# First attention: value products in groups of four, one block later, and ten probability tiles instead of six

## What is computed

```
s1 = einsum('bhtd,bhsd->bhts', q1, k1) * scale + mask     # causal mask
s2 = einsum('bhtd,bhsd->bhts', q2, k2) * scale + mask
diff = softmax(s1) - lam * softmax(s2)
out  = einsum('bhts,bhsd->bhtd', diff, v)                 # 16 heads, v of 32 columns
```

## Time and profile before

| | |
|---|---|
| median of three runs | 972.34 us |
| the profiled execution, its own time | 969.42 us |
| its span | 967.4 us |
| first value product of the first attention, last one | 89.8 us, 415.2 us |
| PE busy | 858.3 us, 89% |
| DVE, ACT, POOL busy | 534.6, 457.4, 450.4 us |

### The profile page before, as it was taken

One profiled execution on the slowest core, in us unless ns is written; L12 is line 12 of the kernel. 1 busy time (PEld: TensorE's weight loads), 2 busy tenths in 40 slices (PEclk: granted clock), 3 DMA queues, 4 the chain that ended last, 5 costly groups with the idle time before them and its releaser, 6 DMA issues. The chain is left out here.

```text
span 967.4 us, 13868 instructions
## 1 busy us (share of the span) xinstructions
PE 858.3 (89%) x4106; PEld 427.3 (44%) x4106; DVE 534.6 (55%) x1498; ACT 457.4 (47%) x981; POOL 450.4 (47%) x893
## 2 busy tenths in 40 slices
PE   3838999999999999979955989898879999999994
PEld 2322433334333333336721233332257777777773
DVE  3738676776766766146366666664024444444445
ACT  1512555555655565722230465665524444444442
POOL 1831646646463443442130233333228677777774
PEclk9966999999999999968885799999779999999998
DMA  5484320000000000010075541112000000000001
GB/s 188 149 259 103 79 67 2 2 2 2 2 2 2 2 2 2 1 38 1 1 218 174 145 138 52 52 51 84 22 30 1 0 0 0 1 0 0 0 1 43
DMA packets 39137, 46.29 MB, mean 48 GB/s; under 512 B 5386, under 2 KB 31339, under 8 KB 39070
## 3 DMA queue, kind: packets, MB, share of 16 engines
q1 hardware_dynamic: 39076, 45.56, 16.3%
HBM read 30.05 MB, written 15.20 MB: 47 GB/s over the span
## 5 line engine op out<-in xcount | busy, mean ns | idle before, releaser
L619 DVE CUSTOM_DVE_ANT_0 ps<-ps,keep 128x512 f32<-128x512 f32 (+3 forms) x384 | 188.7, 500 | 117.7 <-PE ps L487 114.8
L575 ACT ACTIVATE top<-ps 128x512 f32<-128x512 f32 (+3 forms) x384 | 174.7, 491 | 140.7 <-PE ps L498 139.0
L487 PE MATMUL ps<-mid 96*128 96x512 bf16 (+3 forms) x576 | 191.2, 353 | 35.3 <-PEq L898 15.3
L498 PE MATMUL ps<-mid 99*128 99x512 bf16 (+3 forms) x576 | 187.9, 339 | 17.4 <-ACT mid L575 14.3
L518 PE MATMUL ps<-top,mid 128*64 128x512 f32 (+3 forms) x768 | 170.2, 513 | 0.7
L498 PEld LDWEIGHTS ps<-mid 99*128 99x128 bf16 x576 | 56.5, 101 | 212.6 <-ACT top L575 114.8
L1301 PE MATMUL ps<-xp,wp 128*128 128x512 f32 (+1 forms) x600 | 144.7, 390 | 0.0
L575 ACT ACTIVATE mid<-ps 128x512 f32<-128x512 f32 (+1 forms) x192 | 87.3, 490 | 91.4 <-PE ps L518 50.7
L1301 PEld LDWEIGHTS ps<-xp,wp 128*128 128x128 f32 (+1 forms) x600 | 111.9, 187 | 24.9 <-issue 0.5
L735 POOL TENSOR_SCALAR_AFFINE_SELECT top<-top 128x128 f32<-128x128 f32 x256 | 73.1, 298 | 103.5 <-ACT top L575 101.6
L1438 DVE SCALAR_TENSOR_TENSOR a<-th,ps 128x512 f32<-128x512 f32 (+1 forms) x50 | 34.4, 688 | 115.4 <-ACT th L1367 115.4
(11 more groups left out here) (204 smaller groups left out, 1003.5 us busy)
## 6 DMA issues: line engine op xcount, KB each, us to landing
mid<-part_scratch SPq DMA_DIRECT2D x9, 1152.0 KB, 8.5
part_scratch<-top SPq DMA_DIRECT2D x18, 384.0 KB, 3.4
top<-in_w SPq DMA_DIRECT2D x16, 396.0 KB, 3.9
part_scratch<-top SPq DMA_DIRECT2D x18, 256.0 KB, 3.4
mid<-part_scratch SPq DMA_DIRECT2D x9, 384.0 KB, 4.1
top<-in_w SPq DMA_DIRECT2D x8, 384.0 KB, 4.7
part_scratch<-top SPq DMA_DIRECT2D x18, 128.0 KB, 3.3
keep<-in_x SPq DMA_DIRECT2D x1, 1024.0 KB, 5.5
```

Source lines behind the costliest of these rows:

```text
L487: ins = nc.tensor.matmul(bank[:, 0:w], queries(pair, m)[0:PARTS, i * P:(i + 1) * P], keys(pair, m)[0:PARTS, c * 512:c * 512 + w], start=Tr ...
L498: nc.tensor.matmul(ps[:, ST_BANK + n % AHEAD, 0:w], keys(pair, m)[0:STACK, j * P:(j + 1) * P], queries(pair, m)[0:STACK, q0:q0 + w], start ...
L575: nc.scalar.activation(pr[:, n % RING, 0:w], ps[:, ST_BANK + n % AHEAD, 0:w], ACT.Exp, scale=0.25).then_inc(p_ready, 1)
L619: ins = nc.vector.tensor_tensor_reduce(bank, bank, msk[:, 512 - w:512], -1.0 if low else 1.0, 3e38 if low else -3e38, ALU.add, ALU.min if ...
```

## The change

The first attention gets ten tiles of `pr` instead of six and groups of four value products instead of two. A group is issued at the steps n = 5, 9, 13, ... and holds the blocks n - 5 to n - 2; before, it was issued at n = 2, 4, 6, ... and held n - 2 and n - 1. The four products left at the end are issued behind the loop. The second attention keeps its numbers (`RING` 6, `VGROUP` 4, `LAG` 0). Nothing changes on the other engines.

```diff
-                RING = 6
-                VGROUP = 2 if first else 4
+                RING = 10 if first else 6
+                VGROUP = 4
+                LAG = 1 if first else 0
...
-                            if n > 0 and n % VGROUP == 0:
-                                for done in range(n - VGROUP, n):
+                            if n > LAG and n % VGROUP == LAG:
+                                for done in range(n - LAG - VGROUP, n - LAG):
                                     value_step(done)
```

## The result

The changed kernel takes 994.67 us (median of 4 runs, 992.92 to 998.55); the kernel before 970.48 us, the median of its three earlier runs and one more of 966.97. The ratio of the mean times is 1.026 with a 95% interval of 1.021 to 1.031: slower by 24 us. The forecast was 996, from 984 to 1006. The profiled execution took 998.55 us with a span of 996.5, so it is 29.1 us longer than the one of before.

What follows compares the result with a forecast made beforehand. PE alone bounds the first attention. Per pair -1.5 + 2.05 + 1.17 + 0.15 = +1.87 us, +29.9 over 16 pairs; less 0.8 and 4.4, +24.7 on 969.42 gives 994.1; with 2.9 for the median, forecast 996, range 984 to 1006.

Steps and rivals of the forecast that it cites:

- The switch: First attention, PE between bf16 and value products: 0.25 us per group, paid once per four; 1.5 us per pair saved.
- The copies: First attention, ACT's copies at steps 9 and 1 delay exponentials PE needs: 1.0, 0.84 and 0.2, together 2.05 us per pair.
- The gaps: First attention, bf16 steps behind groups of four: PE waits for ACT, two score blocks ahead at most; 1.17 us per pair.
- DVE's bank at step 21: First attention, step 21: the maximum product waits for the bank of the one three before; 0.15 us per pair.
- PE's busy share near 85%: Expected sign in the profile after: PE's busy share in the first attention's windows, with the clock at 1.00.
- The masks: First attention, pairs with quantisation: later issue gives POOL's masks more time; 0.87 us for each of five, 4.4 us saved.
- POOL would no longer release L518: Expected sign in the profile after: POOL no longer a releaser of L518, the value products, in the first attention.
- The ends: First attention's first pair and loop end: no late half to copy, -0.8 us; four products left, 0.6 us, within rounding.
- Rival 4: First attention: PE's clock falls as PE idles 3.4 of 22.4 us per pair; 27 us on top, 1023; chance 0.04.
- Rival 1: First attention: nothing takes the place of what is removed, ACT and DVE have room; 944 us; chance 0.03.
- Rival 2: First attention: the copies' wait is hidden and only the gaps between groups stay; 963 us; chance 0.03.
- Rival 3: First attention: only the copies cost, the gaps are filled; 975 us, or 972 if the first copy is cheap; chance 0.05.

Runs made afterwards that it cites:

- the first experiment: Against the changed kernel, each copy L584 of the first attention stands one exponential later in ACT's order; 974.07 us, ratio 1.007 to the kernel before.

## Why the prediction was right, point by point

**The switch.** Right: 0.09 us ahead of a group and 0.16 behind, once per four products. Six groups fewer save 1.5 us per pair.

**The copies.** Right. At step 11 the prediction had 1.0 us, the trace 0.99; at step 3 it had 0.84, the trace 0.83 (312.76 to 313.59); at step 5 0.2 against 0.20. That it is the copy's place and not the group's length is shown by two kernels that differ in that alone, once with groups of four (22.31 to 20.99 us per pair) and once with groups of two (22.48 to 20.64).

**The gaps.** Right. The trace has 0.31 and 0.09 behind step 13, 0.24 and 0.04 behind step 17, 0.31 and 0.10 behind step 21, and 0.14 us for DVE's bank at step 21: 1.23 us against 1.32. (For that bank I had written 0.15, though the two times beside it, 1.2 and 1.16, differ by 0.04 only: the size was right, its working was not complete.) All waits of a pair sum to 3.25 us, and 20.50 - 1.5 + 3.25 = 22.25 stands against the 22.31 measured.

One sign did not come: PE's busy share near 85%. The window shows 92%, 44.09 of 48 us. PE idles 3.25 of 22.31 us from start to start, 15%, but a matmul's modelled end lies past the point where the next one could start (0.39 us long at 512 columns, where the next starts after 0.23), so a part of each wait counts as busy.

**The masks.** Right in effect: all pairs have one length. Wrong in what would show it. I wrote that POOL would no longer release L518; the waits still list it, and not less than before. From 120 to 425 us:
```profile
PEld ps L519 <- POOL top L736: 11.7, 45, 0.3
```
In the window of the earlier trace rows, 120 to 400 us, it is 10.7 us and 41 times against 10.5 and 29. The weight load is free well before the group is due, and what the profile names is the last event before it. From the end of the bf16 product's columns to the group are 0.09 to 0.11 us in all six groups of the pair above. The line tells of PEld's idle time, not of PE's. Before, the 0.87 us lay at the groups of steps 22, 0 and 2 (233.56, 235.16 and 236.67 us), whose masks stood behind POOL's steps L752 and L755 of 1.26 and 1.04 us. The relief needs no lag: without it, too, all pairs have one length, 21.30 us.

**The ends.** Mis-sized. I gave the last pairs the same cost as all others, 1.87 us each. Over the 14 pairs up to step 11 of the one before the last, the trace has +21.1 us (291.3 to 312.4), against 14 x 1.87 - 4.35 = 21.8. From there to the last `sel_step` it takes 33.2 us instead of 26.9: +6.3, where my sum had 2.9 for both ends together. Two things are in it. No maximum products are left there, which gave a stretch bound by PE 3.1 us per pair back: before, the last whole pair takes 17.35 us. After, it takes 22.30 (406.48 to 428.78), since ACT's waits give none of this back, they only grow. PE's rows there, from steps 16 and 0:
```profile
414.97 0.34 PE L499 MATMUL ps<-mid 99*128 99x384 bf16 x1 [0.47 <-ACT top L576]
...
421.52 0.34 PE L499 MATMUL ps<-mid 99*128 99x384 bf16 x1 [0.47 <-ACT top L576]
```
And PE's clock fell once between the first `sel_step` and the last, in a stretch with such waits (windows, columns as in the earlier trace rows):
```profile
420.00:425.00 5.00, 3.25 (x19) 1.08 (x15) 0.00 (x0) 3.20 (x8) 1.45 (x5) 0.98 0.00 0
425.00:428.78 3.78, 3.77 (x12) 1.18 (x12) 0.00 (x0) 0.42 (x3) 0.83 (x3) 0.58 0.02 4
```
PE was busy 3.25 of 5 us, and then a group took 3.17 us at a granted clock of 0.58, where the same one otherwise takes 1.73: 1.4 us. Rival 4 was right about the kind and far off in size; the 0.04 that it had was for 27 us.

So the profiled execution grew by 29.1 us where I had 24.7, and the medians by 24.2. Of the 29.1, 27.4 lie between the first and the last `sel_step`, 0.2 ahead of them, and 1.5 behind, where the code is the same and nothing in my sum stood. The agreement of 994.67 with 996 is in part luck. I added 2.9 us for the distance of the first median to its profiled run, while the profiled run after lies 3.9 above its own median. And 994.1 + 2.9 is 997.0: the 996 is a slip of 1 us, towards what was measured; the rivals' times that start from 996 are 1 us low as well.

**The rivals.** Rival 1 (nothing takes the place) needs both waits away; even with the copies moved, groups of four everywhere stay 6 us above before. Rival 2 (copies' wait hidden by itself) did not happen, and with the copies moved the time was 974, not 963, because the new waits of 0.4 and 0.2 us come in. Rival 3 (gaps filled) is refuted by the rows above.

## What to carry to other kernels

Before you move a producer later in one engine's order, look at every instruction of the other engines that waits on it, and at what stands behind that instruction in its own order: here two copies of 0.6 us, which had been free, held up the exponential that PE needed two steps on, at 2 us a pair. A saving on the engine that sets the pace counts only as far as its partners can keep it fed without it, and the time between two groups matters there, not their size. Merge where something else already fills that time, and move the waiting instruction along with what it waits for: that turned +2.6% into -0.8%.

## What I had not expected of the hardware

The eight f32 products of a `sel_step` take 0.84, 0.89 or 0.95 us to the next product, by what stands ahead of them: 512 columns of bf16, 128 columns, or a group. Behind an idle PE they take 0.94 as well (308.96 to 309.90 in the first experiment). The weight loads go with it: the first load of L538 starts 0.22 us ahead of its product behind the 512 columns (219.57 and 219.79), 0.06 us ahead behind the 128 (223.58 and 223.64), and together with it behind a group (304.48) or an idle PE (308.96). That this is the cause is not shown.

And PE's granted clock fell inside a stage in which PE never pauses for more than 1.1 us at a time: to 0.50, the lower of its two levels (1.2 GHz), from 425 to 428 us, after 5 us with PE busy at 65%. It stayed at 1.00 where PE was busy at 92%, and was at 1.00 again in the 15 us up to the last `sel_step`, with PE busy at 82%. With the copies later it fell once too (0.75 and 0.91 in the windows from 404 to 409 and to 414 us); in the other kernels it stayed at 1.00 from the first `sel_step` to the last.
